# Expert rows loaded behind the group six back with the filling rows in four lots, and rotary attention's memory values added by a product of 128 rows

## The chip, the cores and the metric

One core of one Trainium2 chip runs the whole kernel. The metric is the device time of one execution in microseconds. PE is the matrix engine, DVE, ACT and POOL are the vector, scalar and GpSimd engines, SP is the queue that issues most DMAs. In a row, "PEld" is the load of weights into PE's array and "SPq" the instruction queue of SP.

## What is computed

A block of four sublayers on x of 8 x 512 x 256, each added to x. Two of them are touched here, the rotary attention of layer 1 and the mixture of experts that ends the kernel:

```python
# rotary attention: persistent memory rows stand ahead of keys and values
q, k, v = (split_heads(q), split_heads(k), split_heads(v))
q = apply_rope(q)
k = apply_rope(k)
pm = jnp.broadcast_to(persist_mem[None], (b, heads, n_pm, dim_head))
k = jnp.concatenate([pm, k], axis=2)
v = jnp.concatenate([pm, v], axis=2)
...
# experts
router_logits = jax.nn.sigmoid(x @ gate_w + gate_b)
expert_values, expert_indices = jax.lax.top_k(router_logits, k=TOP_K)
expert_values = expert_values / jnp.sum(expert_values, axis=-1, keepdims=True)
hg = jnp.einsum('bsd,edi->bsei', x, experts_wg)
hu = jnp.einsum('bsd,edi->bsei', x, experts_wu)
all_outputs = jnp.einsum('bsei,eid->bsed', jax.nn.silu(hg) * hu, experts_wd)
selected = jnp.take_along_axis(all_outputs, expert_indices[..., None], axis=2)
expert_weighted = jnp.sum(expert_values[..., None] * selected, axis=2)
return x + _mlp(x, shared_wg, shared_wu, shared_wd) + expert_weighted
```

Sixteen attention heads of 64 with 4 memory rows; sixteen experts, two of them for each of the 4096 tokens.

## The kernel before

The kernel is a chain of stages, each a block of programs for the five engines with a barrier behind it. Matrices are split into two halves of 16 bit (a high part and the rest), so that each product is three products.

**Rotary attention** (`attention_stage`, L1165, which hands its tiles to `attention_core`, L761). The unit of work is a pair of heads of one batch: 64 pairs, some 13 us each. A slot of the loop works on several pairs at once, shifted against each other: while PE sums the weighted values of pair s-1, it makes the scores of pair s+1 and the projections of pair s+2. `rope_slot` writes out the order on each engine by hand. On PE a slot runs through `scores` (waits for DVE's maxima of the part before), then mostly `project_values`, `scores_T`, `project` and `values`; DVE's `normalise` (L1019) waits for the last `values`. `project_values` makes four tiles of 128 tokens x 128 columns, each of six products of 128 rows (L838). The first tile has the four memory rows in it. They come in by one more product (L840), `identh` by `pmv`: `pmv` holds the memory values of each pair, high part in rows 0 to 3, low part in rows 32 to 35, zero elsewhere, and `identh` has ones at the same rows. Both tiles have 36 rows (`PMR`, L1177). `identh` is cleared by POOL and `pmv` by DVE before the loop (L1265, L1235).

**Experts** (`expert_stage`, L1978). The stage before has written every token's row (256 values as high and low parts, the place of its result and its gate) into a table in memory, `rows_dram`, sorted by expert. The stage works through 80 tiles of 128 rows in 20 groups of four: 16 groups of full tiles, whose experts are read from a table at run time (`name_experts`), then 4 groups with the last, partly filled tile of each expert. Where such a tile has no token, a filling row must stand: 16 indirect DMAs of POOL write 128 filling rows each (L2022), before SP may load group 16.

A group g goes this way. SP loads four tiles of 129 KB (L2005) into buffer g%6 of `xt`. PE turns them (`turn`, L2034), ACT and DVE copy them to `xT`, PE makes the gate and up products (`upward`, L2052), ACT and DVE the activation, PE the down product (`downward`, L2060). ACT and DVE scale the result into one of four buffers of `yt`, and POOL scatters it to `found_dram` by four indirect DMAs (L2026); they also read the places from `xt`, so that the buffer is free only when they have landed. PE's order is turn(g+1), upward(g), downward(g-1), turn(g+2) and so on. At the end, when all scatters have landed, SP reads the results back in eight parts, DVE adds them and SP stores the output.

SP may load group g, from the seventh on, when a semaphore of `scattered` has risen far enough. There are four of these, one for each g%4, and the wait of L2002 reads `scattered[g%4]` with the count `(g-6)//4+1`. For groups 6, 7, 10, 11, 14, 15, 18 and 19 this means the scatter of the group four back (2, 3, 6, 7 and so on); for groups 8, 9, 12, 13, 16 and 17 it means the group eight back, which has long been done. POOL writes all filling rows first and then waits for group 0.

Of the kernel before, what the change touches and what calls it, by code (L numbers as in the profile page):

```python
# [5 lines left out]
P=128  # L6
# [4 lines left out]
NB,T,D,NH=8,512,256,256  # L11
C=16
I=128; NE=16; NX=NE+1
HEADS,DH,PM=16,64,4
PAIRS=HEADS//2
# [19 lines left out]
@contextmanager  # L35
def semaphores(nc, stage):

    taken=[]
    def take(name):
        taken.append(nc.alloc_semaphore(name=stage+name))  # L40
        return taken[-1]
    yield take
    nc.clear_and_free_semaphores(taken)
    nc.all_engine_barrier()
# [1126 lines left out]
def attention_stage(nc, XT, HT, w_qkvT, w_outT, pmT, pmV, rope, ident, tails):  # L1171

    with ExitStack() as ctx:
        sb=lambda n,s,d=F32: ctx.enter_context(nc.sbuf_tensor("att_"+n,s,d))
        sem=ctx.enter_context(semaphores(nc,"att_"))

        PMR=32+PM  # L1177
        w=sb("w",[P,2,2,3*INNER_],F16)
        wo=sb("wo",[P,2,PAIRS,D],F16); tab=sb("rope",[P,2,T]); pmk=sb("pmk",[P,PAIRS,2,PM],F16); pmv=sb("pmv",[PMR,PAIRS,P],F16)
        after=sb("after",[P,2,P],BF16); afterT=sb("afterT",[P,2,P],BF16); ones=sb("ones",[P,P],BF16); identb=sb("identb",[P,P],BF16); identh=sb("identh",[PMR,P],F16)  # L1180
        with ExitStack() as c1:
            sb1=lambda n,s,d=F32: c1.enter_context(nc.sbuf_tensor("attw_"+n,s,d))
            NCH=3*INNER_//512; ORDER=(4,5,0,1,2,3); TR=NB*PM
# [795 lines left out]
def expert_stage(nc, XT, HT, ident, wall, tile_row, last_row, group_experts, pad, pad_row, rows_dram, found_dram, out):  # L1979

    NT=NB*T//P; REGION=NB*T+P; FULL=2*NT; MAXT=FULL+NE; ROW=D+2; I32=mybir.dt.int32
    base=HT[:,:,:,:].rearrange("p k b t -> p (k b t)").rearrange("p (j d) -> p j d",d=D)
    room=XT[:,:,:,:].rearrange("p k b t -> p (k b t)")
    with ExitStack() as c2:
        sb2=lambda n,s,d=F32: c2.enter_context(nc.sbuf_tensor("exp_"+n,s,d))
        sem2=c2.enter_context(semaphores(nc,"exp_"))
        G=4; NG=MAXT//G; NF=FULL//G; NC=NT//G; XB=6; YB=4
        ps=lambda n,s,d=F32: c2.enter_context(nc.psum_tensor("exp_"+n,s,d))
        px=[ps(f"turned{i}",[P,2,4,P],F16) for i in range(2)]; ph=[ps(f"hg{i}",[P,512]) for i in range(2)]; pu=[ps(f"hu{i}",[P,512]) for i in range(2)]; pd=[ps(f"out{i}",[P,2,D]) for i in range(2)]
        identh=sb2("identh",[P,P],F16)  # L1990
        xt=sb2("xt",[P,XB,G,ROW],I32); xT=sb2("xT",[P,2,G,4,P],F16); si=sb2("silu",[P,2,512]); tg=sb2("tg",[P,2,512]); hid=sb2("hid",[P,2,2,512],F16)
        ob=sb2("ob",[P,2,G,D])
        found=room[:,0:4*G*D].rearrange("p (u c j d) -> p u c j d",u=2,c=2,d=D); yt=room[:,4*G*D:(4+YB)*G*D].rearrange("p (u j d) -> p u j d",u=YB,d=D)
        idh=sem2("identh"); loaded=[sem2(f"loaded{i}") for i in range(XB)]; turned=sem2("turned"); xt_kept=[sem2(f"turned_kept{i}") for i in range(2)]; up_done=sem2("up_done"); silu=sem2("silu"); product=sem2("product"); hi=sem2("hi"); lo=sem2("lo"); down=sem2("down"); y_kept=[sem2(f"y_kept{i}") for i in range(2)]; scattered=[sem2(f"scattered{i}") for i in range(YB)]
        pads_sent=sem2("pads_sent"); back=[sem2(f"back{i}") for i in range(2)]; paired=sem2("paired"); summed=sem2("summed"); stored=[sem2(f"stored{i}") for i in range(2)]
        block=c2.enter_context(nc.Block())
        def words(g,d): return xt[:,g%XB].bitcast(d)
        @block.sync
        def _(sp):
            for g in range(NG):  # L2000
                if g==NF: sp.wait_ge(pads_sent,16*NE)
                if g>=XB: sp.wait_ge(scattered[g%YB],16*G*((g-XB)//YB+1))  # L2002
                for i in range(G):
                    r=sp.value_load(tile_row[g*G+i:g*G+i+1,0:1] if g<NF else last_row[0:1,(g-NF)*G+i:(g-NF)*G+i+1],min_val=0,max_val=NE*(REGION+P)-P)  # L2004
                    sp.dma_start(xt[:,g%XB,i],rows_dram[bass.ds(r,P),:]).then_inc(loaded[g%XB],16)  # L2005
            for i in range(YB): sp.wait_ge(scattered[i],16*MAXT//YB)
            def store(m):
                sp.wait_ge(summed,m+1)
                for b in range(NB):
                    sp.dma_start(out[b,m*G*C:(m+1)*G*C,:].rearrange("(j t) d -> t j d",t=C),ob[b*C:(b+1)*C,m%2]).then_inc(stored[m%2],16)  # L2010
            for m in range(NC):
                if m>=2: sp.wait_ge(paired,m-1)
                for c in range(2):
                    at=c*NB*T+m*G*P
                    sp.dma_start(found[:,m%2,c],found_dram[at:at+G*P,:].rearrange("(j q) d -> q j d",q=P)).then_inc(back[m%2],16)
                if m: store(m-1)
            store(NC-1)
            for i in range(2): sp.wait_ge(stored[i],16*NB*NC//2)
        @block.gpsimd
        def _(pool):  # L2020
            for e in range(NE):
                nc.gpsimd.indirect_dma_start(rows_dram[:,:],bass.IndirectOffsetOnAxis(pad_row[:,e:e+1],0),pad[:,e,:],None).then_inc(pads_sent,16)  # L2022
            for g in range(NG):
                for i in range(G):
                    if i%2==0: pool.wait_ge(y_kept[i//2],g+1)
                    nc.gpsimd.indirect_dma_start(found_dram[:,:],bass.IndirectOffsetOnAxis(words(g,U32)[:,i,D:D+1],0),yt[:,g%YB,i],None).then_inc(scattered[g%YB],16)  # L2026
# [158 lines left out]
def build(nc, a, out):  # L2185

    with ExitStack() as ctx:
# [33 lines left out]
        cond1_stage(nc,XT,HT,g)  # L2221
        late.close()
        attention_stage(nc,XT,HT,a["L1_attn_w_qkvT"],a["L1_attn_w_outT"],a["L1_attn_memory_keys"],a["L1_attn_memory_values"],a["rope"],ident,tails_dram)

        wall=sb("expert_weights",[P,2,NX,3*D],F16); tile_row=sb("tile_row",[P,1],mybir.dt.int32); last_row=sb("last_row",[P,NE],mybir.dt.int32); group_experts=sb("group_experts",[1,2*NB*T//P//4],mybir.dt.int32)
        pad=sb("pad_rows",[P,NE,D+2],mybir.dt.int32); pad_row=sb("pad_row",[P,NE],U32)
        rnn_dispatch_stage(nc,XT,HT,a["L1_cond2_Wx"],a["L1_cond2_Wh"],a["L1_cond2_b"],h0T,*[a["L1_ffn_"+n] for n in ("gate_w","gate_b","shared_wg","shared_wu","shared_wd","experts_wg","experts_wu","experts_wd")],ident,wall,tile_row,last_row,group_experts,pad,pad_row,rows_dram)
        expert_stage(nc,XT,HT,ident,wall,tile_row,last_row,group_experts,pad,pad_row,rows_dram,found_dram,out)


# [36 lines left out]
```

## Time and profile before

| | us |
|---|---|
| median of three runs | 3782.42 (3779.88 to 3782.56) |
| the profiled execution | 3805.44 |
| its span, first to last instruction | 3803.5 |
| rotary attention's pairs, from about 2083 to 3031 of the span | 948 |
| expert stage, first load issued to last scatter landed, 3532.9 to 3748.2 | 215.3 |
| reading back, adding and storing, 3748.2 to 3803.5 | 55.3 |

All times of rows are microseconds from the start of the span of the profiled execution, which took 23.0 us longer than the median; differences between places in it are used, and the sum is taken off the median. PE is busy 83% of the span, DVE 59%, ACT 44%, POOL 32%; these are means over stages with different limits, and each stage has to be read by itself.

### The profile page before, as it was taken

The page shows a single profiled execution, that of the slowest core. Times are in us where ns is not written, and L with a number is a line of the kernel's source. Part 1 is how long each engine was busy: PE and PEld are TensorE (multiplying, and loading weights), DVE is VectorE, ACT ScalarE, POOL GpSimd, SP SyncE. Part 2 cuts the span into 40 slices and gives each one's busy share as a digit, 9 for nine tenths or more (in the row PEclk, how much of TensorE's full clock was granted, in tenths as well). Part 3 has the DMA queues.
Part 4 walks back from the last instruction along what each step waited for, and adds up shares of the span by engine and source line. Part 5 has one row for each costly group of instructions (what it writes and reads, how often), then busy time and mean ns, then how long its engine had stood idle before and what let it go on. Part 6 is the DMA issues. An engine that isn't in the chain of part 4 may idle for free. (4 is left out here: it accounts for less than half of the span.)

```text
span 3803.5 us, 143700 instructions
## 1 busy us (share of the span) xinstructions
PE 3140.8 (83%) x58958; PEld 2400.2 (63%) x58958; DVE 2247.7 (59%) x6777; ACT 1692.0 (44%) x5164; POOL 1216.8 (32%) x1533
## 2 busy tenths in 40 slices
PE   8677488988889889689985899999999889999571
PEld 5545278888888888545532666666666567777451
DVE  4667644444444444478865888889888745555233
ACT  2179333333333333366743555556555534444230
POOL 0032410000000000133311655566555544443342
PEclk9899755555555555599997999999999955555786
DMA  4011110000000000011001000000000010110335
GB/s 133 1 55 46 31 26 14 14 25 14 25 14 14 25 14 25 15 33 25 17 1 52 2 2 3 2 3 3 2 3 2 16 51 30 32 33 28 109 102 173
DMA packets 110725, 116.07 MB, mean 31 GB/s; under 512 B 52782, under 2 KB 94199, under 8 KB 110112
## 3 DMA queue, kind: packets, MB, share of 16 engines
q1 hardware_dynamic: 102416, 87.33, 8.1%
q0 software_dynamic: 7824, 21.46, 1.6%
q8 instruction: 403, 6.60, 0.7%
q14 instruction: 82, 0.67, 0.1%
HBM read 79.62 MB, written 29.13 MB: 29 GB/s over the span
## 5 line engine op out<-in xcount | busy, mean ns | idle before, releaser
L676 PE MATMUL banks<-hp,whp 128*128 128x8 f16 x24576 | 741.6, 168 | 117.5 <-DVE hp L743 117.5
L676 PEld LDWEIGHTS banks<-hp,whp 128*128 128x128 f16 x24576 | 698.0, 104 | 178.2 <-DVE hp L743 169.4
L709 ACT ACTIVATE ig<-banks 128x32 f32<-128x32 f32 x512 | 100.9, 197 | 577.2 <-PE banks L676 577.2
L738 DVE SCALAR_TENSOR_TENSOR carry<-ig 128x16 f32<-128x16 f32 x512 | 91.6, 179 | 424.9 <-ACT ig L709 424.9
L646 POOL COPY HT<-hist 128x128 f32 x64 | 21.2, 407 | 986.6 <-DVE hp L748 986.6
L1088 ACT ACTIVATE att_PH<-att_stp 128x1024 f16<-128x1024 f32 (+3 forms) x258 | 183.2, 710 | 325.4 <-PE att_stp L888 325.4
L1753 PE MATMUL rnn_banks<-rnn_hp,rnn_whp 128*128 128x8 f16 x6144 | 285.4, 171 | 40.3 <-ACT rnn_hp L1811 15.4
L1753 PEld LDWEIGHTS rnn_banks<-rnn_hp,rnn_whp 128*128 128x128 f16 x6144 | 248.3, 107 | 107.1 <-ACT rnn_hp L1811 76.1
L1007 DVE TENSOR_TENSOR att_PL<-att_P,att_PH 128x1024 f16<-128x1024 f32 (+3 forms) x257 | 266.3, 1075 | 0.5 <-issue 0.2
L654 PE MATMUL banks<-xs,wxp 128*128 128x64 f16 x3168 | 263.7, 241 | 0.0
L1147 POOL TENSOR_TENSOR att_QK<-att_rot,att_QK 128x512 f16<-128x512 f32 x133 | 174.2, 1310 | 239.6 <-ACT att_QK L1080 239.6
L1905 DVE TENSOR_TENSOR rnn_hp<-rnn_hist,rnn_hp 128x16 f16<-128x16 f32 x512 | 97.7, 191 | 227.6 <-ACT rnn_hist L1812 218.7
L1811 ACT ACTIVATE rnn_hp<-rnn_banks 128x16 f16<-128x16 f32 x512 | 93.7, 183 | 279.5 <-PE rnn_banks L1753 277.4
L832 PE MATMUL att_pj<-att_hT,att_w 128*128 128x512 f16 x804 | 201.0, 386 | 17.4 <-POOL att_hT L1151 15.6
L990 DVE TENSOR_REDUCE att_mx<-att_sp 128x2 f32<-128x264 f32 (+3 forms) x263 | 209.6, 818 | 1.1 <-PE att_sp L862 1.1
L1138 POOL TENSOR_TENSOR att_ab<-att_ab,att_rope 128x512 f32<-128x512 f32 x134 | 169.8, 1267 | 124.2 <-DVE att_ab L980 123.4
L1142 POOL TENSOR_TENSOR att_rot<-att_ab 128x512 f32<-128x512 f32 x134 | 204.2, 1524 | 14.8
L654 PEld LDWEIGHTS banks<-xs,wxp 128*128 128x128 f16 x3168 | 194.5, 126 | 0.0
L1093 ACT ACTIVATE att_P<-att_stp 128x1024 f32<-128x1024 f32 (+3 forms) x258 | 180.6, 700 | 5.3 <-DVE att_PL L1007 5.3
L901 PE MATMUL att_acc<-att_V,att_PH 128*128 128x65 f16 (+1 forms) x3584 | 180.0, 193 | 0.0
L743 DVE TENSOR_TENSOR hp<-og,tc 128x16 f16<-128x16 f32 x512 | 90.1, 176 | 144.2 <-ACT tc L715 144.2
L901 PE MATMUL att_acc<-att_V,att_PL 128*128 128x65 f16 x1792 | 175.0, 192 | 0.0
(606 smaller groups left out, 7712.9 us busy)
## 6 DMA issues: line engine op xcount, KB each, us to landing
gen_w<-in_L_cond_W_dram SPq DMA_DIRECT2D x32, 512.0 KB
exp_xt<-expert_rows_scratch SPq DMA_DIRECT2D x80, 129.0 KB
edge_cb<-cols_scratch SPq DMA_DIRECT2D x16, 512.0 KB, 3.8
XT<-expert_found_scratch SPq DMA_DIRECT2D x16, 512.0 KB, 4.9
mod_xn<-in_x_dram SPq DMA_DIRECT2D x8, 512.0 KB
XT<-in_xT_dram SPq DMA_DIRECT2D x1, 4096.0 KB
out_dram<-exp_ob SPq DMA_DIRECT2D x64, 64.0 KB, 2.2
attw_st<-in_L_attn_w_qkvT_dram SPq DMA_DIRECT2D x6, 512.0 KB
```

The source lines that it names most:

```text
L654: last=nc.tensor.matmul(out, wxp[:,wpart,k,col:col+128], xs[:,st,xpart,k,steps], start=False,stop=False,skip_group_check=True)
L676: last=nc.tensor.matmul(out, whp[:,wpart,k,col:col+128], hp[:,k,hpart], start=False,stop=True,skip_group_check=True)
L832: last=nc.tensor.matmul(pj[:,:],c_.w_of(n)[:,wpart,k,col:col+P],h_of(n)[:,xpart,k,PM:PM+T],start=(i==0),stop=(i==5)); i+=1
L901: last=nc.tensor.matmul(out[:,0:wide],p[:,h,at:at+P],V[:,n%4,tt,part,h,0:wide],start=(tt==0 and a==0 and p is PH and part==0),stop=(tt==(R ...
L990: i=nc.vector.tensor_reduce(out=mx[:,:,qt:qt+1],in_=s_ps[:,:,at:at+w_],axis=X_AX,op=ALU.max); at+=w_
L1007: i=nc.vector.tensor_tensor(PL[:,:,at:at+w_],P32[:,t%2,:,0:w_],PH[:,:,at:at+w_],ALU.subtract)
L1088: nc.scalar.activation(PH[:,:,at:at+w_],st_ps[:,:,0:w_],ACT.Exp,scale=DH**-0.5)
L1093: i=nc.scalar.activation(P32[:,t%2,:,0:w_],st_ps[:,:,0:w_],ACT.Exp,scale=DH**-0.5)
L1138: nc.gpsimd.tensor_tensor(ab[:,1],ab[:,1],c_.tab[:,1],ALU.mult).then_inc(turned,1)
L1142: nc.gpsimd.tensor_tensor(rot_of(j),ab[:,0],ab[:,1],ALU.add).then_inc(summed,1)
L1147: nc.gpsimd.tensor_tensor(dst[:,1],rot_of(j),dst[:,0],ALU.subtract).then_inc(lo,1)
L1753: last=nc.tensor.matmul(pre(st,par)[:,u,j], whp[:,wpart,k,u*P:u*P+P], hp[:,k,hpart], start=False,stop=True,skip_group_check=True)
```

## The change

Three edits.

1. The two tiles of the memory product get 128 rows in place of 36; the rows added are zero. The product stays one instruction.
2. SP's load of group g waits for `scattered[(g-6)%4]`, with the same count: for every group from the seventh on, this is the scatter of the group six back, the one that used the same buffer.
3. The sixteen DMAs of filling rows are issued in four lots of four, one ahead of the scatters of each of groups 0 to 3. Ahead of lot g, POOL waits until PE has turned group g+1 (`turned` at 2(g+2)).

```diff
@@ -1176,8 +1176,8 @@
-        wo=sb("wo",[P,2,PAIRS,D],F16); tab=sb("rope",[P,2,T]); pmk=sb("pmk",[P,PAIRS,2,PM],F16); pmv=sb("pmv",[PMR,PAIRS,P],F16)
-        after=sb("after",[P,2,P],BF16); afterT=sb("afterT",[P,2,P],BF16); ones=sb("ones",[P,P],BF16); identb=sb("identb",[P,P],BF16); identh=sb("identh",[PMR,P],F16)
+        wo=sb("wo",[P,2,PAIRS,D],F16); tab=sb("rope",[P,2,T]); pmk=sb("pmk",[P,PAIRS,2,PM],F16); pmv=sb("pmv",[P,PAIRS,P],F16)
+        after=sb("after",[P,2,P],BF16); afterT=sb("afterT",[P,2,P],BF16); ones=sb("ones",[P,P],BF16); identb=sb("identb",[P,P],BF16); identh=sb("identh",[P,P],F16)
@@ -1984,7 +1984,7 @@
-        G=4; NG=MAXT//G; NF=FULL//G; NC=NT//G; XB=6; YB=4
+        G=4; PG=4; NG=MAXT//G; NF=FULL//G; NC=NT//G; XB=6; YB=4
@@ -1999,7 +1999,7 @@
             for g in range(NG):
                 if g==NF: sp.wait_ge(pads_sent,16*NE)
-                if g>=XB: sp.wait_ge(scattered[g%YB],16*G*((g-XB)//YB+1))
+                if g>=XB: sp.wait_ge(scattered[(g-XB)%YB],16*G*((g-XB)//YB+1))
@@ -2018,9 +2018,11 @@
         def _(pool):
-            for e in range(NE):
-                nc.gpsimd.indirect_dma_start(rows_dram[:,:],bass.IndirectOffsetOnAxis(pad_row[:,e:e+1],0),pad[:,e,:],None).then_inc(pads_sent,16)
             for g in range(NG):
+                if g<PG:
+                    pool.wait_ge(turned,2*(g+2))
+                    for e in range(g*NE//PG,(g+1)*NE//PG):
+                        nc.gpsimd.indirect_dma_start(rows_dram[:,:],bass.IndirectOffsetOnAxis(pad_row[:,e:e+1],0),pad[:,e,:],None).then_inc(pads_sent,16)
                 for i in range(G):
                     if i%2==0: pool.wait_ge(y_kept[i//2],g+1)
```

## Rows read from the trace of the kernel before

**Rows 1.** Stages by window: stretch, length, busy us (count) by engine, clock, DMA.
```profile
3748.00:3803.50 55.50, 0.00 (x0) 0.00 (x0) 19.59 (x16) 0.00 (x0) 0.00 (x0) 0.50 0.81 227
```

**Rows 2.** Timeline of PE, the four stops; start, length, instruction, idle before it.
```profile
3599.89 1.89 PE L2034 MATMUL exp_turned<-exp_identh,exp_xt 128*128 128x128 f16 x16 [11.05 <-DMA exp_xt<-expert_rows_scratch]
...
3638.99 1.89 PE L2034 MATMUL exp_turned<-exp_identh,exp_xt 128*128 128x128 f16 x16 [9.45 <-DMA exp_xt<-expert_rows_scratch]
...
3679.18 1.89 PE L2034 MATMUL exp_turned<-exp_identh,exp_xt 128*128 128x128 f16 x16 [10.63 <-DMA exp_xt<-expert_rows_scratch]
...
3717.03 1.89 PE L2034 MATMUL exp_turned<-exp_identh,exp_xt 128*128 128x128 f16 x16 [10.55 <-DMA exp_xt<-expert_rows_scratch]
```

**Rows 3.** Chain of waits in the expert stage, ahead of the second stop.
```profile
3629.55 2.41 DMA expert_found_scratch<-XT,exp_xt
3631.98 0.27 SPq L2004
...
3636.02 2.93 DMA exp_xt<-expert_rows_scratch
3638.99 1.03 PE exp_turned L2034 x8
```

**Rows 4.** Timeline of PE, groups 3 and 5 turned without a stop.
```profile
3566.35 1.06 PE L2034 MATMUL exp_turned<-exp_identh,exp_xt 128*128 128x128 f16 x16
...
3581.11 1.06 PE L2034 MATMUL exp_turned<-exp_identh,exp_xt 128*128 128x128 f16 x16
```

**Rows 5.** Timeline of POOL: first scatters of groups 0 and 16, last scatter.
```profile
3568.11 0.96 POOL L2026 DMA_INDIRECT expert_found_scratch<-XT,exp_xt  x1 [15.59 <-ACT XT L2078]
...
3725.34 0.96 POOL L2026 DMA_INDIRECT expert_found_scratch<-XT,exp_xt  x1 [11.40 <-ACT XT L2078]
...
3745.72 0.96 POOL L2026 DMA_INDIRECT expert_found_scratch<-XT,exp_xt  x1 [0.30 <-issue]
```

**Rows 6.** Timeline of SP, loads: beside filling, behind it, beside a scatter of group 7.
```profile
3538.11 16.30 SPq L2005 DMA_DIRECT2D exp_xt<-expert_rows_scratch  x6
...
3555.32 12.93 SPq L2005 DMA_DIRECT2D exp_xt<-expert_rows_scratch  x12
...
3632.69 3.66 SPq L2005 DMA_DIRECT2D exp_xt<-expert_rows_scratch  x4
```

**Rows 7.** Timeline of PE, groups 1 and 2 turned.
```profile
3545.61 1.89 PE L2034 MATMUL exp_turned<-exp_identh,exp_xt 128*128 128x128 f16 x16 [4.65 <-DMA exp_xt<-expert_rows_scratch]
...
3559.23 1.89 PE L2034 MATMUL exp_turned<-exp_identh,exp_xt 128*128 128x128 f16 x16 [0.87 <-DMA exp_xt<-expert_rows_scratch]
```

**Rows 8.** Waits of the expert stage: us in total, times, longest.
```profile
PE exp_turned L2034 <- DMA exp_xt<-expert_rows_scratch: 64.7, 7, 17.5
...
PE exp_hu L2052 <- issue: 5.0, 4, 1.9
```

**Rows 9.** Scatters by line: ns of one, min/median/max.
```profile
L2026 POOL DMA_INDIRECT expert_found_scratch<-XT,exp_xt x80: 954/960/1337, 3568.1 to 3745.7; - x80
```

**Rows 10.** Timeline of ACT, activations of groups 2 and 3.
```profile
3573.95 0.60 ACT L2085 ACTIVATE exp_silu<-exp_hg 128x512 f32<-128x512 f32 x1 [5.20 <-remote]
...
3582.62 0.60 ACT L2085 ACTIVATE exp_silu<-exp_hg 128x512 f32<-128x512 f32 x1 [5.05 <-remote]
```

**Rows 11.** Timeline of PE in rotary attention, around one memory product.
```profile
2507.32 0.51 PE L838 MATMUL att_vo<-att_w,att_hT 128*128 128x128 f16 x6
2507.76 0.23 PE L840 MATMUL att_vo<-att_pmv,att_identh 36*128 36x128 f16 x1
2507.91 1.18 PE L838 MATMUL att_vo<-att_w,att_hT 128*128 128x128 f16 x18
```

**Rows 12.** Waits of rotary attention's loop, 2083 to 3030 us.
```profile
DVE XT L1028 <- PE att_pj L915: 79.5, 8, 9.9
...
PE att_sp L857 <- DVE att_mx L991: 55.4, 58, 2.4
...
DVE att_inv L1019 <- PE att_acc L901: 13.1, 44, 0.3
```

## The prediction

> **What bounds the kernel now.** I read the page's shares first, and they say little: PE is busy most of the span, but the three edits lie in two stages, and each is bound in its own way. So I took the windows of the stages, then each engine's timeline in them, then the waits.
>
> In the expert stage PE works in stretches. Its timeline shows four stops ahead of a `turn` [rows 2], of 11.05, 9.45, 10.63 and 10.55 us, together 41.7. Each ends with a load, and each stands ahead of a group whose load waits for the scatter of the group four back (6, 10, 14, 18). With the waits at the start of the stage they make up the 64.7 us that PE waits for loads [rows 8]. The chain of waits tells what a stop is made of [rows 3]: the last scatter of group 6 is issued at 3629.55 and lands 2.4 us later, SP issues four loads up to 3636.0, the last lands, and PE turns group 10 at 3638.99: 9.4 us in series from the last scatter's issue. The reader should see that no engine is the limit. It is a circle of four groups: load, turn, products, scatter, next load. Its length is the pace of the scatters, from 3568.11 (group 0) to 3725.34 (group 16) [rows 5]: 157.2 us for 16 groups, 9.83 a group, 39.3 for four. Between stops PE needs less: groups 3 and 5 are turned 14.76 us apart [rows 4], 7.4 a group.
>
> In rotary attention PE and DVE wait for each other in a slot: PE for DVE's maxima (58 times, 55.4 us), and DVE for PE's weighted values (44 times, 13.1 us) [rows 12]. Between these two waits lies an unbroken stretch of PE with the memory product in it.
>
> **Edit 1, the memory product.** In a stream of 128-row products one starts every (1.18-0.22)/17 = 0.056 us; 0.22 is the length of one. The sixth product ahead of the memory product starts at 2507.32+0.51-0.22 = 2507.61. The memory product follows at 2507.76 and the next at 2507.91 [rows 11]: 0.30 where two steps of a uniform stream take 0.11. Each of the 66 memory products so costs 0.19 us in going to 36 rows and back; that is 12.5 us of PE. With 128 rows both gaps should be those of the stream. All 64 in the loop would pay if PE alone were the path. They pay only where PE's stretch is: the 44 slots in which DVE waits at its end, on average 0.30 us, more than the 0.19 it gets back, and the 8 output slots in which DVE waits up to 9.9 us for PE [rows 12]. 52 x 0.19 = 10 us. Bounds: 0 if DVE is next at once, 12.5 if all are on the path. I take 10, as DVE's wait covers the gain. What is late next in a slot is DVE itself. The larger clearing is the same number of elements per partition, and lies ahead of the loop beside the loads of the weights: nothing.
>
> The Trainium skill ("TensorE: Matmul & The Clock Gate", "Why this matters for your kernels") speaks against this edit: a single product of 32 rows takes the same time as one of 128, so that filling up rows would give nothing. The row agrees on the product itself, 0.23 against 0.22, but the gaps on both sides are three times those of the stream [rows 11]. The Trainium skill, "TensorEngine Tiling (Array Packing)", "Key Properties", has the reason, that a change of the row tiling drains the array. By the first rule alone the edit gives 0.
>
> **Edit 2, the wait of SP.** The circle becomes one of six groups with the same content: 39.3/6 = 6.5 us a group, below PE's 7.4. So PE's flow sets the pace, the load has some 6 x 7.4 - 39.3 = 5 us of margin, and the four stops go: -41.7. What is late next is PE's own issue. Behind SP's wait stand only later loads; nothing is queued that was free before, since groups 8, 9 and so on came behind 6 and 7 in the same queue. The other buffers hold: results go to a buffer of the group four back, whose scatter at 7.4 a group has landed long before. POOL needs four scatters of 0.96 with 0.30 between, 5.05 a group, and does not bind, except at the end: the last groups are quicker on PE, and POOL closes the stage one scatter after another as now [rows 5]. The 55.5 us of reading back stay [rows 1].
>
> One thing I can't read off: the flow has never lasted longer than three groups. ACT's activations of groups 2 and 3 start 8.67 us apart [rows 10], though PE issues every 7.4, so that ACT falls behind within a stretch and catches up in the stop. If this lag grows, PE has to wait for it. I allow 3 us; bounds 0, and 12 groups x (8.67-7.4) = 15.
>
> **Edit 3, the filling rows.** Now they go out in one go at the start of the stage, and it starts slowly beside them. SP issues its fifth to tenth load in 16.30 us, 2.7 each, against the next 12 in 12.93, 1.08 each, behind them [rows 6]. PE waits 4.65 us for group 1 and 0.87 for group 2 [rows 7], and its products stumble four times without a releaser, 5.0 us together [rows 8]; groups 1 and 2 are turned 13.6 us apart. With the lots behind the turning of group 1, group 1's loads go at 1.08, which is worth about 1.9, and the 5.0 and 0.9 go as well: 7.8. Bounds: 7.8 if lots of four leave the others alone, 0 if each lot costs its share wherever it stands. The first four loads were out before SP slowed down, so short lots should disturb less than the one long one: I take 6.
>
> The price is on POOL. Lots 1 to 3 stand between scatters: POOL has 10.1 us a group there against 7.4 of flow, so that scatters 1, 2, 3 come 2.7, 5.4 and 8.1 us late, and it then catches up 2.3 a group. The results' buffers have the room; the load of group 9 waits for scatter 3 and has 5 us of margin: 3 us, call it 2. The wait for `turned` costs nothing, since POOL has nothing to scatter before group 0 is done. Group 16's wait for the filling rows is met some 70 us early.
>
> The Trainium skill ("DMA: Bandwidth & Descriptors", "SWDGE vs HWDGE vs iDMA") warns that GpSimd builds its descriptors in memory that DVE can lock it out of, and the lots now stand beside DVE's copies. The rows of the scatters, which always had DVE beside them, don't show it: 0.954, 0.960 and 1.337 us at least, in the middle and at most [rows 9]. By the rule 16 issues would stretch by a DVE copy each; by the row, by nothing.
>
> **The sum.** -41.7 + 3 - 6 + 2 - 10 = -52.7. The profiled execution took 3805.44, its span 3803.5; that gives 3752.7. It ran 23.0 us above the median of 3782.42, and nothing says the stops are part of that: the circle is made of transfers and waits. 3782.4 - 52.7 = 3729.7.
>
> **The rivals.**
> - *DVE takes the place at once in rotary attention* (edit 1 gives 0): 3740. For it: DVE's idle time in a slot is small. Against: 44 waits of 0.30. Chance 0.15.
> - *The flow runs at ACT's pace of 8.67*: 12 us worse, 3742. For it, rows 10; against it, that PE never waited for ACT within a stretch. Chance 0.17.
> - *POOL's unbroken work disturbs the flow.* From scatter 0 on POOL issues 28 DMAs without a pause, 35 us. If SP and PE stumble in it as they did at the start, 5 us in each 16, and edit 3 brings nothing: 3729.7 + 6 + 11 = 3747. Chance 0.12.
> - *Slower: SP becomes the bound.* Loads at 2.7 us each beside POOL's DMAs would be 10.9 a group; over 20 groups that is 218 us for the loads alone, where loads and products now take 215, and with a start and an end of 20 us it gives 3782 + 20 = 3802. It decides against the change from about 9.8 us a group on. Against it: beside a scatter four loads took 3.66 us [rows 6]. Chance 0.02.
> - *The wait was not what held the loads*, or the change is not what it says: within 2 us of now but for edit 1. Against it, the four stops with the same chain. Chance 0.02.
>
> **How the numbers follow.** Forecast 3730, chance 0.52, its own range 3720 to 3738. Range: the low end takes the upper bounds (no lag, 7.8, no POOL price, 12.5): 3782.4 - 62 = 3720, and 4 below for stops that are longer without the profiler: 3716. The high end takes in the rivals up to 3747, with 2 more where two of them overlap: 3749. Faster by over 0.2% (7.6 us, about what a measurement of this kernel can tell from no change): 0.96; within: 0.02; slower: 0.02.
>
> **What would show it.** Right: no stop over 2 us ahead of `turn` of groups 6, 10, 14, 18; first scatters of groups 0 and 16 about 118 us apart instead of 157; group 1 turned before 3544 on the old scale; the memory product 0.056 us from both neighbours, and DVE's wait for PE's values near 0.1. Wrong: stops that move to group 9 (POOL's price), scatters 8.7 us apart (ACT's lag), loads of over 2 us each. If PE waits more for DVE's maxima by what it saved, edit 1 was hidden. The forecast fails most if the flow can't be kept over more than three groups.

## The result, and the profile of the changed kernel

| | us |
|---|---|
| before, median of 4 runs | 3781.15 (3779.59 to 3782.56) |
| changed, median of 4 runs | 3754.23 (3752.57 to 3754.86) |
| ratio | 0.9928, 95% interval 0.9911 to 0.9945 |
| the profiled execution of the changed kernel, and its span | 3752.57, 3750.6 |

The kernel became 27 us faster, where 52.7 were forecast, and lies above the range of 3716 to 3749. Profile against profile the difference is 3805.4 - 3752.6 = 52.8, as forecast. That is luck, as the runs below show: the profiled execution of before was 23 us above the runs beside it, while that of the changed kernel is within 2 us of its own. What the profile of before showed was true of that execution and not of the runs that the forecast was about.

PE's timeline in the expert stage of the changed kernel; the columns are start, length, instruction, and in brackets the idle time before it:

```profile
3538.57 1.86 PE L2036 MATMUL exp_turned<-exp_identh,exp_xt 128*128 128x128 f16 x16 [16.60 <-DMA exp_xt<-expert_rows_scratch]
3542.93 1.89 PE L2036 MATMUL exp_turned<-exp_identh,exp_xt 128*128 128x128 f16 x16 [2.50 <-DMA exp_xt<-expert_rows_scratch]
3549.13 1.06 PE L2036 MATMUL exp_turned<-exp_identh,exp_xt 128*128 128x128 f16 x16
...
3603.72 1.89 PE L2036 MATMUL exp_turned<-exp_identh,exp_xt 128*128 128x128 f16 x16 [3.58 <-DMA exp_xt<-expert_rows_scratch]
3610.89 1.06 PE L2036 MATMUL exp_turned<-exp_identh,exp_xt 128*128 128x128 f16 x16
...
3653.97 1.06 PE L2036 MATMUL exp_turned<-exp_identh,exp_xt 128*128 128x128 f16 x16
```

These are the turnings of groups 0, 1, 2, 9, 10 and 16. The four stops of [rows 2] are gone. Groups 1 and 2 are turned 4.4 and 10.6 us after group 0, where [rows 7] had 6.5 and 20.1. A stop of 3.58 us is new, ahead of group 9, as the prediction named it for POOL's price. From group 9 to 16 a group takes (3653.97-3603.72)/7 = 7.18 us. Where the stop comes from, POOL's timeline shows:

```profile
3558.32 0.96 POOL L2028 DMA_INDIRECT expert_found_scratch<-XT,exp_xt  x1 [8.47 <-ACT XT L2080]
...
3568.75 0.96 POOL L2028 DMA_INDIRECT expert_found_scratch<-XT,exp_xt  x1 [0.30 <-issue]
...
3578.86 0.96 POOL L2028 DMA_INDIRECT expert_found_scratch<-XT,exp_xt  x1 [0.30 <-issue]
...
3589.11 0.96 POOL L2028 DMA_INDIRECT expert_found_scratch<-XT,exp_xt  x1 [0.30 <-issue]
...
3673.17 0.96 POOL L2028 DMA_INDIRECT expert_found_scratch<-XT,exp_xt  x1 [0.30 <-issue]
...
3692.80 0.96 POOL L2028 DMA_INDIRECT expert_found_scratch<-XT,exp_xt  x1 [0.30 <-issue]
```

The first four are the first scatters of groups 0 to 3: 10.1 to 10.4 us apart, since a lot of four fillings lies between them, against a flow of 7.2. The scatters of groups 1 to 3 so are 3, 6 and 9 us behind their results. The load of group 9 waits for the last scatter of group 3, issued at 3592.91. The last two rows are the first scatter of group 16 and the last scatter of all; groups 0 and 16 are 114.9 us apart, where [rows 5] has 157.2 and the forecast had 118.

In rotary attention PE's timeline around the memory product that [rows 11] shows:

```profile
2509.81 0.51 PE L838 MATMUL att_vo<-att_w,att_hT 128*128 128x128 f16 x6
2510.15 0.22 PE L840 MATMUL att_vo<-att_pmv,att_identh 128*128 128x128 f16 x1
2510.21 1.17 PE L838 MATMUL att_vo<-att_w,att_hT 128*128 128x128 f16 x18
```

The sixth product starts at 2509.81+0.51-0.22 = 2510.10, the memory product 0.05 behind it, the next one 0.06 behind that: both gaps are those of the stream, as forecast. And yet the loop over the 64 slots, from the first normalising (L1019) to the last, takes 902.0 us instead of 895.6.

### The profile page after: what moved, and what is told of

It reads as the page before. It is cut to its first block and busy times, and to the rows that moved or that the text cites. A ratio compares the mean times of both kernels' runs of the same rounds, so it can differ in the third digit from the quotient of the medians.

```text
span 3750.6 us, 143700 instructions
## 1 busy us (share of the span) xinstructions
PE 3123.9 (83%) x58958; PEld 2390.2 (64%) x58958; DVE 2264.0 (60%) x6777; ACT 1690.7 (45%) x5164; POOL 1228.7 (33%) x1533
## 5 line engine op out<-in xcount | busy, mean ns | idle before, releaser
L1147 POOL TENSOR_TENSOR att_QK<-att_rot,att_QK 128x512 f16<-128x512 f32 x133 | 186.0, 1399 | 217.7 <-ACT att_QK L1080 217.7
```

The lines of the kernel that those rows point to most:

```text
L1147: nc.gpsimd.tensor_tensor(dst[:,1],rot_of(j),dst[:,0],ALU.subtract).then_inc(lo,1)
```

## The experiments

The kernels were measured in five sets ("calls" in the expectations), each on one chip and beside the kernel before. The five sets had five chips, and the medians of the kernel before in them were 3779.1, 3813.4, 3814.7, 3811.4 and 3778.3. This turned out to be the main finding. I call the first and the last chip, on which the kernel takes the time of the table above, the first kind, the other three the second kind. TensorE's granted clock doesn't tell them apart: the runs of the kernel before have a mean of 0.744 to 0.747 on the first kind and 0.742 to 0.747 on the second. No chip was measured in two sets, so the runs don't show whether the kind belongs to the chip or to the time at which a set was run; "kind of chip" below is meant with this reserve.

### First set: each edit alone (first kind, before 3779.1)

Theories P and S in the expectations of this set are about the profiled execution of before: by P something made its expert stage longer than it is in the plain runs, by S the stage was true and the stops are what the profile shows. H and G are about edit 1.

Edit 1 alone is the first two changed lines of the diff.

> Edit 1 alone: the memory product with 128 rows. Both theories leave the expert stage alone here. Theory H (hidden and given back): in 12 of 63 slots a DVE instruction of 4 x 8 elements falls behind a POOL instruction and takes 1.1 instead of 0.15 us, which costs more than the other slots gain: plain time 3 to 8 us longer than before, first to last normalise about 902 us against 895.6. Theory G (the gain is there): 5 to 10 us shorter. The profile decides how many of the 4 x 8 instructions take over 1 us: 12 under H.

Measured: 3782.91 (11 runs), ratio 1.0013 (1.0004 to 1.0022): 3.8 us slower, the loop takes 902.2 us, and 12 of the 64 small instructions take 1.12 us: theory H in all three numbers. DVE's wait for PE's values [rows 12] goes from 0.30 to 0.10 us each. In the spacing of the normalisings 51 slots gain 5.5 us together, many of them going from 12.91 to 12.77, and 12 slots lose 12.0 us together, going from 12.91 to between 13.78 and 13.99. In each of these 12 stands one of the 12 long instructions. In the changed kernel the same slots grow, and there a slot of this sort looks like this, DVE first and POOL below:

```profile
2179.76 1.04 DVE L1007 TENSOR_TENSOR att_PL<-att_P,att_PH 128x520 f16<-128x520 f32 x2
2180.72 1.12 DVE L1010 TENSOR_TENSOR att_PL<-att_P,att_PH 4x8 f16<-4x8 f32 x1
2181.76 0.67 DVE L979 TENSOR_TENSOR att_ab<-att_pj,att_rope 128x512 f32<-128x512 f32 x1
```

```profile
2180.40 1.42 POOL L1147 TENSOR_TENSOR att_QK<-att_rot,att_QK 128x512 f16<-128x512 f32 x1 [1.21 <-ACT att_QK L1080]
```

In the kernel before, the same pair of instructions starts together, and the small one is short:

```profile
2181.22 0.15 DVE L1010 TENSOR_TENSOR att_PL<-att_P,att_PH 4x8 f16<-4x8 f32 x1
```

```profile
2181.22 1.18 POOL L1147 TENSOR_TENSOR att_QK<-att_rot,att_QK 128x512 f16<-128x512 f32 x1 [1.53 <-ACT att_QK L1080]
```

L1010 subtracts the four memory rows of a tile: 4 x 8 elements, 0.15 us. In the changed kernel POOL's instruction starts 0.3 us ahead of it instead of together with it, and DVE's small instruction ends, at 2181.84, when POOL's does, at 2181.82. Both instructions read two tiles of SBUF. The Trainium skill, "SBUF — State Buffer", "SBUF: two separate sides", has the rule: DVE and GpSimd share a pair of ports, and of a DVE instruction with two SBUF inputs and a GpSimd instruction that reads SBUF, whichever starts first holds them to its end, while the other blocks fully. The rows agree, to 0.02 us.

Edit 2 alone is one line:

```diff
-                if g>=XB: sp.wait_ge(scattered[g%YB],16*G*((g-XB)//YB+1))
+                if g>=XB: sp.wait_ge(scattered[(g-XB)%YB],16*G*((g-XB)//YB+1))
```

> Edit 2 alone: SP's load waits for the group six back. Theory P (the profiler lengthened the stage): the execution without a profile has stops of some 6 us, not 10.4, so the plain time falls by 22 to 30 us, while the profiled one falls by 40 or more. Theory S (the stops are as the profile shows them, and another edit gives time back): plain time falls by 40 to 45 us.

Measured: 3744.15 (4 runs), ratio 0.9911 (0.9896 to 0.9926), 34.9 us faster, between the ranges of P and S. This one line alone beats the whole change by 8 us, each taken against the kernel before beside it. No stop is left behind group 1, and the flow is 7.2 us a group over 16 groups: it can be kept.

Edit 3 alone is the hunks with `PG`.

> Edit 3 alone: the filling rows in four lots of four. Theory P: the slow start of the stage is the profiler's as well; plain time within 3 us of before, profiled time up to 20 us shorter. Theory S: plain time 6 to 8 us shorter. If POOL's later scatters cost more with the wait for the group four back, plain time up to 8 us longer.

Measured: 3785.79 (10 runs), ratio 1.0019 (1.0009 to 1.0028), 6.7 us slower, the last case of the expectation. The stop ahead of group 6 is 13.54 us, where edit 1 alone has 7.04:

```profile
3584.73 1.89 PE L2036 MATMUL exp_turned<-exp_identh,exp_xt 128*128 128x128 f16 x16 [13.54 <-DMA exp_xt<-expert_rows_scratch]
```

Group 6's load waits for the scatter of group 2, which is behind its lot. The start, where the gain was to be, is hardly quicker: from the turning of group 0 to that of group 2 it takes 10.65 us here and 11.04 in edit 1 alone, whose fillings go out in one go.

The fourth kernel leaves out the groups, the fillings and the reading back.

> The kernel before without the expert groups: no loads, products, scatters, filling rows or reading back; DVE copies the shared part and SP stores it. Its time stands for all that comes ahead of the groups. Theory P: the profiled execution is within 3 us of the plain one, so that the 23 us between profiled and plain in the kernel before lie in the groups. Theory S: the profiled one is again some 20 us longer.

Measured: 3562.08 (4 runs), 3563.29 profiled, as theory P had it. The stage so is worth 3779.1 - 3562.1 = 217.0 us without a profiler. By the traces (first copy to DVE's last instruction) it lasts 25.5 us in this kernel, 243.6 in edit 1 alone, and 265.2 in the profile of before: differences of 218.1 and 239.7. The profile of edit 1 alone, whose expert code is that of before, fits the plain runs; that of before is 22 us too long in this stage. In edit 1 alone the four stops are:

```profile
3583.70 1.89 PE L2034 MATMUL exp_turned<-exp_identh,exp_xt 128*128 128x128 f16 x16 [7.04 <-DMA exp_xt<-expert_rows_scratch]
...
3621.10 1.89 PE L2034 MATMUL exp_turned<-exp_identh,exp_xt 128*128 128x128 f16 x16 [7.58 <-DMA exp_xt<-expert_rows_scratch]
...
3657.16 1.89 PE L2034 MATMUL exp_turned<-exp_identh,exp_xt 128*128 128x128 f16 x16 [7.17 <-DMA exp_xt<-expert_rows_scratch]
...
3693.42 1.89 PE L2034 MATMUL exp_turned<-exp_identh,exp_xt 128*128 128x128 f16 x16 [9.38 <-DMA exp_xt<-expert_rows_scratch]
```

31.2 us together, where [rows 2] has 41.7. A stop costs more than its own length, which fits the 34.9 of edit 2: PE's clock, granted at 1.00 (2.4 GHz) in the flow, is granted at 0.50 (1.2 GHz) in the 4 us behind the stop of 7.04. The first of these two rows is edit 1 alone, the second edit 2 alone over ten groups; the number ahead of the last two is the granted clock:

```profile
3583.70:3587.70 4.00, 4.00 (x38) 4.00 (x39) 0.69 (x1) 1.02 (x1) 0.00 (x0) 0.50 0.25 75
```

```profile
3572.30:3644.80 72.50, 69.91 (x762) 53.91 (x760) 27.57 (x51) 28.70 (x50) 38.40 (x40) 1.00 0.49 147
```

From their turning to the next one, groups 6, 10, 14 and 18 take 3.1 us more together in edit 1 alone than in edit 2 alone.

I took the profiler for the cause of the longer stage in the profile of before, or a disturbed execution. The next set was to show it.

### Second set (second kind, before 3813.4)

> The kernel before, unchanged, for a second profile. Theory D: the first profile of it was a disturbed execution, and nothing in the kernel makes it so. Then this profile is within 5 us of the time without a profiler (about 3779), the expert stage has the length that it has in the run of edit 1 alone (243.6 instead of 265.2 us), the four stops are 7 to 9.5 us each, about 31 together, and group 2 is turned about 11 us after group 0 (20.1 in the first profile). Theory K: this kernel takes the profiler badly, every time. Then the profiled time is again near 3800, the stops near 10.4 each, and the recorder's effect on the two kernels is to be told from the times alone.

Measured: 3811.43 profiled. Both theories fall. The stage is long again (272.0 us), but the kernel takes as long without the profiler, in 16 of 16 runs (3811.1 to 3817.8): it was not the profiler. Three stretches by the traces, each begun and ended at the same instructions in every row, in us:

| | rotary attention | recurrent stage | experts |
|---|---|---|---|
| profile of before | 979.0 | 486.3 | 265.2 |
| edit 1 alone, first kind | 983.1 | 478.1 | 243.6 |
| before again, second kind | 978.7 | 486.3 | 272.0 |
| edit 2 alone, first kind | 980.1 | 478.7 | 210.5 |
| edit 2 alone, second kind | 980.2 | 487.2 | 249.3 |

The profile of before bears both marks of the second kind, the 8 us more in the recurrent stage and the long expert stage, though its stage is still 7 us under the others of that kind. The plain times beside it are those of the first kind. The record doesn't say whether they ran on one chip with it; if they did, the kind isn't a property of the chip.

> Edits 2 and 3 together, without edit 1. Theory L (the lots cost what they save and more): the lots between the scatters make scatters 1 to 3 late, load 9 waits for scatter 3, and a stop of 3 to 4 us comes before the turning of group 9; the time is about 3750, 6 over edit 2 alone (3744). Theory M (the lots are free, and the whole distance of the changed kernel from edit 2 alone is edit 1): 3744, with no stop before group 9.

Measured: 3801.41 (6 runs), ratio 0.9965 (0.9953 to 0.9977). Edit 2 alone was not in this set, so the price doesn't come out of it; the third set has the pair.

The seventh kernel has edit 1, and the small subtraction goes first:

```diff
-                i=nc.vector.tensor_tensor(PL[:,:,at:at+w_],...,ALU.subtract)
                 if rope and t==QT-1:
-                    at=written(QT)
-                    i=nc.vector.tensor_tensor(PL[0:PM,:,at:at+PM],...,ALU.subtract)
-                i.then_inc(p_low,1)
+                    tail=written(QT)
+                    nc.vector.tensor_tensor(PL[0:PM,:,tail:tail+PM],...,ALU.subtract)
+                nc.vector.tensor_tensor(PL[:,:,at:at+w_],...,ALU.subtract).then_inc(p_low,1)
```

> Edit 1, and the subtraction of the 4 memory rows issued ahead of the large subtraction of its tile instead of behind it; nothing is left out. Theory C (the loss of edit 1 is that small instruction waiting for a POOL instruction which by now starts ahead of it): ahead of the large one POOL is idle, no instance of it takes over 0.2 us, the 12 slots of 13.8 to 14.0 us go back to 12.8, the 64 slots take 889.5 instead of 902.1 us (895.6 before), and the time is about 3770, 9 under the kernel before. Theory R (any DVE instruction in that place is held, so another one takes the wait): the 64 slots stay near 902, and the time near 3783.

Measured: 3806.61 (11 runs), ratio 0.9984 (0.9975 to 0.9993), 6.8 us faster. The loop takes 890.4 us (889.5 expected), and no slot is over 13.02 but the output slots. The rows of the small instruction, out of DVE's groups in the loop, first in the changed kernel, then here (times, busy us, mean ns):

```profile
L1010 DVE TENSOR_TENSOR att_PL<-att_P,att_PH 4x8 f16<-4x8 f32 x64 | 21.1, 330 | 0.0
```

```profile
L1009 DVE TENSOR_TENSOR att_PL<-att_P,att_PH 4x8 f16<-4x8 f32 x64 | 11.4, 178 | 0.0
```

Two of the 64 small instructions still take 1.12 us, where none was expected; one lies ahead of the first normalising, the other in an output slot that has grown by 0.07 us. Theory C is shown for the loop, which goes from 902.2 to 890.4 us when one instruction of 0.15 us is moved. In time, edit 1 turns from 3.8 us of loss on the first kind to 6.8 of gain here; the fifth set has what it gives on the first kind.

> Edits 1 and 2 with the small subtraction ahead of the large one, the filling rows in one go as before. Theory C with theory L: 3744 less the 9 that edit 1 then gives, 3735. Theory R: 3748, the 3744 of edit 2 alone and the 4 that edit 1 costs alone.

Measured: 3786.01 (5 runs), ratio 0.9928 (0.9914 to 0.9941). Both numbers were for the first kind of chip; on this one it is 27.4 us faster than before, where 44 was expected. Edit 2 so gives only 20.6 on top of the 6.8 here.

### Third set: the same again, side by side (second kind, before 3814.7)

> The changed kernel, unchanged, beside the kernel before. Theory Q (there are two kinds of chip here: on one the kernel before takes about 3780 and PE's flow is 7.2 us a group, on the other about 3813 and 8.8 a group, whatever the kernel): on the first kind it takes 3754 again, 27 less than before, on the second 3801 + 4 = 3805, only 8 less. Theory V (the gain belongs to the kernel and the chips shift all kernels alike): 27 less than before on either.

Measured: 3807.61 (11 runs), ratio 0.9982 (0.9973 to 0.9991): 7 us faster, not 27. Theory Q.

> Edit 2 alone once more. Theory Q: on the first kind of chip 35 less than before; on the second kind 21 less (the 27.4 of edits 1 and 2 with the small subtraction first, less the 6.8 of edit 1 with it), since the flow there leaves less between itself and the circle of four groups. Theory V: 35 less on either.

Measured: 3792.33 (5 runs), ratio 0.9945 (0.9931 to 0.9958): 22.4 faster. Theory Q. What the second kind does is seen in ACT's timeline, three activations in a row (L2085) in edit 2 alone. First here, then on the first kind:

```profile
3593.30 0.60 ACT L2085 ACTIVATE exp_silu<-exp_hg 128x512 f32<-128x512 f32 x1 [5.22 <-remote]
3602.12 0.60 ACT L2085 ACTIVATE exp_silu<-exp_hg 128x512 f32<-128x512 f32 x1 [5.20 <-remote]
3610.96 0.60 ACT L2085 ACTIVATE exp_silu<-exp_hg 128x512 f32<-128x512 f32 x1 [5.22 <-remote]
```

```profile
3592.73 0.60 ACT L2085 ACTIVATE exp_silu<-exp_hg 128x512 f32<-128x512 f32 x1 [3.58 <-PE exp_hu L2052]
3600.14 0.60 ACT L2085 ACTIVATE exp_silu<-exp_hg 128x512 f32<-128x512 f32 x1 [3.79 <-PE exp_hu L2052]
3607.29 0.60 ACT L2085 ACTIVATE exp_silu<-exp_hg 128x512 f32<-128x512 f32 x1 [3.52 <-PE exp_hu L2052]
```

Here they are 8.83 us apart, there 7.15 to 7.41. And PE's timeline on the second kind has idle times that nothing in the profile releases:

```profile
3610.82 0.55 PE L2034 MATMUL exp_turned<-exp_identh,exp_xt 128*128 128x128 f16 x7 [0.87 <-issue]
3611.90 0.66 PE L2052 MATMUL exp_hg<-exp_xT,expert_weights 128*128 128x128 f16 x6 [0.53 <-issue]
...
3619.67 0.55 PE L2034 MATMUL exp_turned<-exp_identh,exp_xt 128*128 128x128 f16 x7 [0.79 <-issue]
```

"remote" in place of PE's line means that the signal came well after PE's last product had ended, on the second kind by 2.7 to 3.0 us in this flow. The first of PE's idle times in a group begins 0.1 to 0.2 us after the end of POOL's fourth scatter, whose rows in the same trace are:

```profile
3608.91 0.96 POOL L2026 DMA_INDIRECT expert_found_scratch<-XT,exp_xt  x1 [0.30 <-issue]
...
3617.74 0.96 POOL L2026 DMA_INDIRECT expert_found_scratch<-XT,exp_xt  x1 [0.30 <-issue]
```

The clock isn't the cause: from 3593.3 to 3681.0 it is granted at 0.96, against 1.00 over ten groups of the first kind. The two rows of [rows 10] have the same mark and stand 8.67 us apart: the sign that the profile of before was of this kind stood in my own rows, and I read it as ACT falling behind.

> Edits 2 and 3 once more, in one call with edit 2 alone. The lots' price on the same chip: theory L says 6 on the first kind (load 9 waits for scatter 3), 9 on the second kind (the 21 of edit 2 alone less the 12 of both); theory M says 0 on either.

Measured: 3800.29 (5 runs), 8.0 us over edit 2 alone on the same chip. Theory L, near its 9. The start does gain here: from the turning of group 0 to that of group 2 it takes 10.38 us instead of 18.56 with the fillings in one go. The gain is given back and more while the lots stand between the scatters: in the changed kernel on this chip groups 6 and 7 are turned 18.92 us apart, and the longest wait of ACT for PE's signal is 11.0 us.

> Edits 1 and 2 with the small subtraction ahead of the large one, filling rows in one go. On the first kind of chip theory C says 35 + 7 to 9 = 43 less than before, on the second kind 27 less as measured. If edit 1 with the small subtraction first is worth the same on both kinds, this kernel is 7 to 9 under edit 2 alone in this call.

Measured: 3788.54 (5 runs), 26.2 faster than before, and 3.8 under edit 2 alone, not 7 to 9; the runs of the two overlap (3784.4 to 3791.8, and 3788.2 to 3796.1).

### Fourth set: what slows the flow on the second kind (before 3811.4)

> The kernel before. Theory Q (two kinds of chip): either 3779 with an expert stage of 243.6 us and stops of 7 to 9.5 us, or 3813 with 272 and stops near 11; nothing in between. If it comes between the two, the kinds are a scale and not two.

Measured: 3817.69 profiled, its stage 271.6 us. Two kinds, and nothing between them so far but the profile of before.

Three kernels of edit 2 each take one suspect away. Of each edit only the line that matters is shown; the counts that are waited for follow it, and in the first two the reading back takes rows of x:

```diff
-                    nc.gpsimd.indirect_dma_start(found_dram[:,:],...).then_inc(scattered[g%YB],16)
+                    if i==G-1: nc.gpsimd.indirect_dma_start(found_dram[:,:],...).then_inc(scattered[g%YB],16)
```

> Edit 2, with one of the four scatters of each group left out of the other three (three quarters of the scatters aren't made, and the reading back takes rows of x in their place). If the scatters' transfers slow PE's flow on the second kind, the flow goes from 8.8 to about 7.2 us a group there; if not, it stays 8.8. On the first kind it is 7.2 either way.

Measured: 3754.80 (2 runs), ratio 0.9853 (0.9824 to 0.9881), 56.6 under before. The flow is that of the first kind, 71.0 us between the turnings of groups 6 and 16 where edit 2 alone has 88.4 on the second kind and 72.6 on the first, and ACT waits for PE's line again, with nothing "remote":

```profile
3592.09 0.60 ACT L2085 ACTIVATE exp_silu<-exp_hg 128x512 f32<-128x512 f32 x1 [3.54 <-PE exp_hu L2052]
3599.17 0.60 ACT L2085 ACTIVATE exp_silu<-exp_hg 128x512 f32<-128x512 f32 x1 [3.45 <-PE exp_hu L2052]
3606.15 0.60 ACT L2085 ACTIVATE exp_silu<-exp_hg 128x512 f32<-128x512 f32 x1 [3.35 <-PE exp_hu L2052]
...
3620.45 0.60 ACT L2085 ACTIVATE exp_silu<-exp_hg 128x512 f32<-128x512 f32 x1 [3.55 <-PE exp_hu L2052]
```

```diff
-                for i in range(G):
+                for i in range(G if g<XB else 1):
```

> Edit 2, with only the first of the four loads made in the groups from 6 on (the other three tiles keep the rows that lie there, and the reading back takes rows of x). If SP's loads slow PE's flow on the second kind, it goes from 8.8 to about 7.2 us a group from group 6 on; if not, it stays 8.8. On the first kind 7.2 either way.

Measured: 3787.23 (3 runs), ratio 0.9938 (0.9915 to 0.9960), 24.2 under before. Groups 6 and 16 are turned 81.7 us apart, 8.2 a group.

```diff
-                v=pe.value_load(group_experts[0:1,g:g+1],min_val=0,max_val=NE**4-1)
-                experts[g]=[((v>>(4*i))&(NE-1)).with_bounds(min_val=0,max_val=NE-1) for i in range(G)]
+                experts[g]=list(range(g%4*G,(g%4+1)*G))
```

> Edit 2, with the experts of each group fixed in the program instead of read from the table (the choice of experts is left out, so the products take other experts' weights): PE's value load, its register arithmetic and the register moves ahead of the products go. If PE's own stream of instructions sets the 8.8 on the second kind, the flow falls to about 7.2 or less; if the transfers do, it stays 8.8. On the first kind it is at most 0.3 us a group shorter, the products themselves taking some 6.9.

Measured: 3787.49 (3 runs), ratio 0.9930 (0.9906 to 0.9954), 23.9 under before. Groups 6 and 16 are turned 84.1 us apart, 8.4 a group. But it is no even flow: the activations are between 3.5 and 12.3 us apart.

```profile
3624.62 0.60 ACT L2081 ACTIVATE exp_silu<-exp_hg 128x512 f32<-128x512 f32 x1 [5.15 <-remote]
3628.13 0.61 ACT L2081 ACTIVATE exp_silu<-exp_hg 128x512 f32<-128x512 f32 x1
3640.43 0.60 ACT L2081 ACTIVATE exp_silu<-exp_hg 128x512 f32<-128x512 f32 x1 [8.66 <-PE exp_hu L2048]
```

Nor are the products some 6.9 us a group, as the expectation has it. The last four groups, whose experts are fixed in every kernel, are 4.88 apart in edit 2 alone on the first kind. So PE had much less to do here, and yet the flow is hardly faster: PE's register work isn't what sets 8.8.

So, of the three suspects, it is the scatters. With a quarter of them the 8.83 us become 7.1; a quarter of the loads gives back 0.7, and leaving out PE's register work 0.4. Whether it is their issue by POOL or the rows that they move isn't told apart, since both go with a scatter that is left out, and how a scatter delays PE's issue isn't shown. POOL's own row doesn't tell the kinds apart (medians of 960 to 963 ns on the first kind, 959 to 963 on the second). The 8 us of the recurrent stage fit, since POOL issues an indirect DMA per tile there too, but no kernel leaves those out.

### Fifth set (first kind, before 3778.3)

> Edits 1 and 2 with the small subtraction ahead of the large one. On the first kind of chip (before about 3779) 3744 less 5 to 8, so 3736 to 3739; on the second kind 3786 to 3789 again, 4 under edit 2 alone.

> Edit 2 alone. On the first kind 3744, on the second 3792. The loop of rotary attention in it takes 895.6 us against 890.3 with edit 1 and the small subtraction first, so the two kernels should be 5 us apart on either kind.

Measured: 3741.50 (4 runs, ratio 0.9898, 0.9883 to 0.9913) and 3743.02 (5 runs, ratio 0.9910, 0.9896 to 0.9924). The kernel with the small subtraction first is faster than the kernel before and the changed kernel, but only 1.5 us under edit 2 alone and not 5, and 1.5 us can't be told from nothing: the runs of the two overlap. Rotary attention does gain 5.4 us here (979.3 to 973.9), and the stages ahead of it, in which no instruction is changed, lose 5.4: they end at 2057.3 instead of 2051.9. In the three profiles of this kernel rotary attention begins at 2057.0, 2057.4 and 2057.3, in all others between 2051.3 and 2056.1. The others, with the same instructions up to there, differ by 4.8 us among themselves, so it may be chance; whether it is stays open.

## Why the prediction was wrong

Forecast and measured, in us against the kernel before:

| | forecast | first kind | second kind |
|---|---|---|---|
| edit 2 | -38.7 | -34.9, -35.3 | -22.4 |
| edit 3 | -4 | +6.7 alone, +4.2 in the whole | +8.0 beside edit 2 |
| edit 1 | -10 | +3.8 alone | +7.3 beside the others |
| all three | -52.7 | -26.9 | -7.1 |

(+4.2 is what is left of -26.9 after -34.9 and +3.8, which come from another set; +7.3 is 3807.61 - 3800.29. Each has the scatter of two medians.)

Of the 25.8 us between forecast and measurement on the first kind, 13.8 are edit 1, 8.2 edit 3 and 3.8 edit 2. So two steps failed. Edit 1's is the larger: with its -10 the time would have been 3740 and in the range. The other runs through edits 2 and 3 and comes first, since the whole sum was built on it.

**"Nothing says the stops are part of that."** This step of the sum failed. The profiled execution took 23.0 us longer than the median, and I carried every length over as it stood. Against edit 1 alone on the first kind, it was 8.2 us longer in the recurrent stage and 21.6 in the experts', the stage that the change touches. The four stops were 31.2 us on that kind and not 41.7, and group 2 was turned 11 us after group 0 and not 20.1. What made that execution longer bears the marks of the second kind, on which the scatters delay PE's issue. Two rows held the sign: "remote" ahead of ACT's activations [rows 10], and the stumbling of PE without a releaser [rows 8].

**Edit 2.** The mechanism was right in each part: the stops went, no new one came, the flow was kept. The term was -41.7 with 3 back for ACT's lag, and it gave -35. That it came so near is in part luck. The stops were 10.5 us shorter than the term had them, but there is no lag on the first kind, and the groups behind the stops were 3.1 us slower together, at about half the clock (0.50 to 0.53) in their first 4 us, which the term left out. From the first scatter of group 0 to that of group 16 it is 111.3 us instead of the 145.3 of edit 1 alone. On the second kind the rival "the flow runs at ACT's pace of 8.67" came true in its number and not in its cause: 8.83 a group, with PE's signals late.

**Edit 3, the start.** -6 forecast. On the second kind 8 us, my upper bound of 7.8, on the first 0.4 to 0.5, since SP's loads don't slow down beside the fillings there: in edit 1 alone SP issues its fifth to tenth load in 6.8 us, where [rows 6] has 16.30 for the same six. The number was taken from the execution that the median doesn't stand for.

**Edit 3, the price.** I put 2 on it. The steps were right: scatters 3 to 9 us late (2.7 to 8.1 forecast), the load of group 9 behind scatter 3, a stop where it was named, 3.58 us. I had worked out 3 us and put 2. Less the 0.5 us of gain at the start, the rows make +3.1 of edit 3; the plain times have +4.2 in the whole, with the scatter of their medians. On the second kind the runs fit the rival "POOL's unbroken work disturbs the flow": groups 6 and 7 are turned 18.92 us apart, and PE's idle time between them, 9.3 us, is without a releaser.

**Edit 1.** Both gaps closed as computed, 0.19 us a product, and DVE's waits shrank as forecast. The step that failed is "They pay only where PE's stretch is", with no price for what moves: "What is late next in a slot is DVE itself" stopped too early, for I didn't ask which instructions of DVE and POOL would move against each other. POOL's start moved to 0.3 us ahead of a DVE instruction that then waits for its end. 12 slots lost 12.0 us, and the 51 others gained 5.5. The term of -10 was +3.8. With that collision out of the way the loop gains 5.2 us, so that -10 was also twice too large by itself. In time that is -6.8 on the second kind, -3.8 there beside edit 2, and -1.5 beside edit 2 on the first kind, the last not clear of noise.

**The range.** It reached to 3749, each rival alone and two of them overlapping. All three terms were off in the same direction, two of them in part for one reason, so that their errors didn't cancel. None of the rivals had edit 1 costing time.

## What to carry to other kernels

Before a length is taken from a profiled execution, set its own time beside the plain runs; if they differ by more than the runs do among themselves, find the stage that holds the difference, and don't subtract lengths of that stage from the plain time. An edit that shortens one engine's stretch shifts all the others against each other: look for pairs of DVE and POOL instructions with two SBUF operands that start within a few tenths of a microsecond. Indirect DMAs of POOL are best kept few in such a flow: on three of the five chips they cost PE time that their own 0.96 us doesn't show.

## What was not expected of the hardware

- Five chips fall into two kinds for this kernel: 3778.3 and 3779.1, and 3811.4, 3813.4 and 3814.7 us. The difference is 8 us in the recurrent stage and 28 in the experts' (272.0 against the 243.6 of edit 1 alone, whose expert code is the same), none in rotary attention. Each chip was measured at one time only.
- On the second kind PE's flow takes 8.83 us a group with four scatters in each and 7.1 with one (from 3592.09 to 3620.45 for four groups). The three left out give back 1.7 us a group.
- A gain measured on one kind isn't that on the other: 27 and 7 us for the change, 35 and 22 for its best line.
- An instruction of DVE on 4 x 8 elements took 1.12 us instead of 0.15 when a POOL instruction had started 0.3 us ahead of it; issued elsewhere, 62 of 64 take 0.15.
- A stop of 7.04 us of PE is followed by 4 us at half the clock (granted 0.50 against 1.00 in the flow).
